# First cross attention of a decoder: batches in order, scores in three fp32r passes, splits and normalization on POOL

## The reference, cut to what matters

```
kv_rope = kv_c * cos + rotate_half(kv_c) * sin          # [8, 375, 128]
q_r = q_big @ W_qr ; k_r = kv_rope @ W_kr               # per head
scores = q_r @ k_r.T                                    # [8, 16, 112, 375]
attn = softmax(scores)
ctx_c = attn @ kv_rope                                  # [8, 16, 112, 128]
out = (ctx_c through w_kc_kv, per head) @ Wo.T
```

## Time and profile before

| | us |
|---|---|
| median of 3 runs | 1679.07 (1675.69, 1679.07, 1680.11) |
| the profiled execution | 1674.48 |
| its span, first to last instruction | 1672.7 |
| PE busy | 1604.6 (96%) |
| DVE busy | 989.6 (59%) |
| ACT busy | 730.5 (44%) |
| POOL busy | 508.7 (30%) |
| mean granted TensorE clock | 0.992 of 2.4 GHz |

### The profile page before, as it was taken

How to read it: one execution, slowest core, us unless ns; L and a number is a source line. 1 busy time by engine, 2 the same in 40 slices (tenths; PEclk the granted TensorE clock), 3 DMA queues, 4 the chain that set the end, 5 groups by cost and what they waited for, 6 DMA issues and landing times.

```text
span 1672.7 us, 24191 instructions
## 1 busy us (share of the span) xinstructions
PE 1604.6 (96%) x9704; PEld 1332.0 (80%) x9704; DVE 989.6 (59%) x1659; ACT 730.5 (44%) x1222; POOL 508.7 (30%) x335
## 2 busy tenths in 40 slices
PE   7999999999899999989999989999889999999998
PEld 7997667778688888867889987787668888888887
DVE  6555663455667675487758748244767455554554
ACT  2113664322577765666621146432635344353442
POOL 3875542620100002332118634111512432222321
PEclk9999999999899999999999999999999999999999
DMA  4110003133312004410001110111001111111111
GB/s 164 51 64 27 2 2 129 40 109 121 107 51 64 14 1 161 157 38 1 1 0 63 51 39 1 37 51 32 21 1 57 51 51 57 51 45 51 51 57 45
DMA packets 28579, 88.51 MB, mean 53 GB/s; under 512 B 4154, under 2 KB 4282, under 8 KB 28215
## 3 DMA queue, kind: packets, MB, share of 16 engines
q1 hardware_dynamic: 28468, 86.96, 15.5%
HBM read 85.11 MB, written 1.84 MB: 52 GB/s over the span
## 4 chain that ended last, share of the span: by engine, by line
PE 85%; DVE 8%; ACT 5%; issue 1%; POOL 0%; ACTq 0%; DVEq 0%
PE PS L255 17%; PE PS L257 17%; PE PS L256 17%; PE PS L260 6%; PE PS L1040 5%; PE PS L1058 4%; PE PS L1390 3%; PE PS L946 3%; PE PS L1405 2%; PE PS L555 2%; PE PS L579 1%; PE PS L1637 1%; PE PS L1625 1%; PE PS L545 1%; DVE sm L1659 1%
## 5 line engine op out<-in xcount | busy, mean ns | idle before, releaser
L301 POOL TENSOR_TENSOR HL<-stg,HL 128x1024 fp32r<-128x1024 f32 (+2 forms) x111 | 244.6, 2207 | 825.1 <-ACT HL L296 807.1
L255 PE MATMUL PS<-XT,HL 128*128 128x448 f32 x608 | 224.4, 369 | 4.3 <-DVE XT L336 3.7
L256 PE MATMUL PS<-XT,HL 128*128 128x448 f32 x608 | 222.6, 366 | 0.0
L257 PE MATMUL PS<-XT,HL 128*128 128x448 f32 x608 | 222.5, 366 | 0.0
L296 ACT ACTIVATE HL<-stg 128x1024 fp32r<-128x1024 f32 (+2 forms) x111 | 104.2, 944 | 216.0 <-PE PS L257 199.5
L255 PE MATMUL PS<-HL,XT 128*128 128x512 f32 (+1 forms) x380 | 137.5, 362 | 2.2 <-DVE XT L1909 1.4
L257 PE MATMUL PS<-HL,XT 128*128 128x512 f32 (+1 forms) x380 | 134.9, 355 | 0.0
L256 PE MATMUL PS<-HL,XT 128*128 128x512 f32 (+1 forms) x380 | 134.7, 355 | 0.0
L255 PEld LDWEIGHTS PS<-XT,HL 128*128 128x128 f32 x608 | 114.6, 188 | 16.5 <-DVE XT L336 4.9
L256 PEld LDWEIGHTS PS<-XT,HL 128*128 128x128 f32 x608 | 114.7, 189 | 9.1
L257 PEld LDWEIGHTS PS<-XT,HL 128*128 128x128 f32 x608 | 114.6, 188 | 9.2
(11 more groups left out here) (288 smaller groups left out, 3611.9 us busy)
## 6 DMA issues: line engine op xcount, KB each, us to landing
stg<-in_wst SPq DMA_DIRECT2D x87, 512.0 KB, 3.7
stg<-in_wst SPq DMA_DIRECT2D x16, 352.0 KB, 3.3
stg<-in_wst SPq DMA_DIRECT2D x16, 320.0 KB, 3.5
wsum<-in_wfc SPq DMA_DIRECT2D x8, 512.0 KB, 3.9
wsum<-in_wpj SPq DMA_DIRECT2D x8, 512.0 KB, 3.5
raw<-in_wfc SPq DMA_DIRECT2D x8, 512.0 KB, 7.9
stg<-in_wst SPq DMA_DIRECT2D x16, 256.0 KB, 2.8
raw<-in_wpj SPq DMA_DIRECT2D x7, 512.0 KB, 7.0
```

What stands on the lines that cost most here:

```text
L255: e.matmul(out, lh, rh, start=start, stop=False)
L256: e.matmul(out, lh, rl, start=False, stop=False)
L257: return e.matmul(out, ll, rh, start=False, stop=stop)
L301: e.tensor_tensor(slot(k)[:, 1, 0:n], stg[k % NSTG][:, 0:n], slot(k)[:, 0, 0:n].bitcast(F), A.subtract).then_inc(*done("pool_w", k))
```

## The change

The units go batch by batch: unit u is batch u // 8 and heads 2(u % 8), 2(u % 8) + 1. The result of a unit overwrites its own queries (`pair_of`), and queries no longer lie one slot above. The scores are three fp32r passes (`mm3`) of 376 columns (375 keys and one of zeros) in place of a plain fp32 matmul. For this POOL splits the queries of two units at a time (`query_parts`: a copy and a subtraction, 448 elements) and the keys of a batch (`keys_parts`: the same on 375). POOL also multiplies the exponentials by the reciprocal, both heads in one instruction with the reciprocal spread over 375 columns, which DVE did in two. The remainder of weight piece ox 2 is made by POOL in `pool_x` at step 3, behind the product of unit 2, where it was the last of `pool_q`. `pe_x` starts when the splits of batch 0 and of units 0 and 1 are there and the queries are all made; it no longer waits for the rotation of all batches before its first scores. The result pieces 0 to 3 are rounded and subtracted in two parts, batches 0 to 5 at steps 52 to 59, and batches 6 and 7 after the last unit.

```diff
+        QOX, KVX = rQO + 16 * 8 * S * 4, rKV + 24288
+        qxh = [at(f"qxh{i}", [128, 4, S], R, QOX + i * 3584) for i in range(2)]
+        qxl = [at(f"qxl{i}", [128, 4, S], R, QOX + i * 3584 + 1792) for i in range(2)]
+        kxh = [at(f"kxh{i}", [128, L + 1], R, (KVX + 6080, KVX)[i]) for i in range(2)]
+        kxl = [at(f"kxl{i}", [128, L + 1], R, (KVX + 3008, KVX + 1504)[i]) for i in range(2)]
...
         def qx_at(half, h):
-            s = 1 + 8 * (h // 8) + 4 * half
+            s = 8 * (h // 8) + 4 * half
...
             for b in range(NB):
                 rotate_rows(e, b)
-            for i in range(3):
+            for i in range(2):
+                e.tensor_scalar(kxh[i][:, L:L + 1], C("ones")[:, 0:1], 0.0, None, A.mult)
+                last = e.tensor_scalar(kxl[i][:, L:L + 1], C("ones")[:, 0:1], 0.0, None, A.mult)
+            last.then_inc(*done("pool_x", "pad"))
+            keys_parts(e, 0)
+            query_parts(e, 0)
+            for i in range(2):
                 rest_w(e, piece["ox", i][0])
...
+        def keys_parts(e, b):
+            e.wait_ge(*upon("dve_ctx", "k", b if b == 0 else NB - 1))
+            if b > 1:
+                e.wait_ge(*upon("pe_x", "sc", 8 * b - 9))
+            e.tensor_copy(kxh[b % 2][:, 0:L], kvT[:, b, :]).then_inc(*done("pool_x", "kh", b))
+            e.wait_ge(*upon("pool_x", "kh", b))
+            e.tensor_tensor(kxl[b % 2][:, 0:L], kvT[:, b, :], kxh[b % 2][:, 0:L].bitcast(F), A.subtract).then_inc(*done("pool_x", "k", b))
+
+        def pair_of(u):
+            return QO[:, 8 * (u // 4 % 2) + u // 8, 2 * (u % 4):2 * (u % 4) + 2, :]
+
+        def query_parts(e, u):
+            i = u // 2 % 2
+            q = QO[:, 8 * (u // 4 % 2) + u // 8, 4 * i:4 * i + 4, :]
+            if u < 8 or u == 32:
+                e.wait_ge(*upon("dve_q", "o", u + 1 if u < 8 else 7, u // 32))
+                e.wait_ge(*upon("act_q", "o", u + 1 if u < 8 else 7, u // 32))
+            if u > 3:
+                e.wait_ge(*upon("pe_x", "sc", u - 3))
+            e.tensor_copy(qxh[i][:, :, :], q).then_inc(*done("pool_x", "qh", u))
+            e.wait_ge(*upon("pool_x", "qh", u))
+            e.tensor_tensor(qxl[i][:, :, :], q, qxh[i][:, :, :].bitcast(F), A.subtract).then_inc(*done("pool_x", "q", u))
+
+        def pool_x(e):
+            for st in range(UX + 1):
+                if st % 2 == 0 and st + 2 < UX:
+                    query_parts(e, st + 2)
+                if st % 8 == 4 and st // 8 + 1 < NB:
+                    keys_parts(e, st // 8 + 1)
+                if st:
+                    u = st - 1
+                    k = u % 4
+                    e.wait_ge(*upon("dve_x", "rx", u))
+                    e.tensor_tensor(Sx[k][:, :, :], Sx[k][:, :, :], rx[:, k, :].unsqueeze(2).to_broadcast([S, 2, L]),
+                                    A.mult).then_inc(*done("pool_x", "p", u))
+                if st == 3:
+                    rest_w(e, piece["ox", 2][0])
...
         def pe_x(e):
-            e.wait_ge(*upon("dve_q", "o", 7, 1))
-            e.wait_ge(*upon("act_q", "o", 7, 1))
-            e.wait_ge(*upon("dve_ctx", "k", 7))
-            e.wait_ge(*upon("pool_ctx", "k", 7))
             for st in range(UX + 4):
                 if st < UX:
-                    b, bank = st // 4 % 8, 2 * (st % 2)
-                    if st > 1:
+                    b, bank = st // 8, 2 * (st % 2)
+                    if st % 8 == 0:
+                        e.wait_ge(*upon("pool_x", "k", b))
+                    e.wait_ge(*upon("pool_x", "q", st // 2 * 2))
+                    if st < 2:
+                        e.wait_ge(*upon("dve_q", "o", 7, 1))
+                        e.wait_ge(*upon("act_q", "o", 7, 1))
+                    else:
                         e.wait_ge(*upon("act_x", "exp", st - 2))
                     for e_ in range(2):
-                        last = e.matmul(PS[0:S, bank + e_, 0:L], QO[:, 1 + st // 4, 2 * (st % 4) + e_, :], kvT[:, b, :],
-                                        start=True, stop=True)
+                        i, j = st // 2 % 2, 2 * (st % 2) + e_
+                        last = mm3(e, PS[0:S, bank + e_, 0:L + 1], qxh[i][:, j, :], qxl[i][:, j, :], kxh[b % 2][:, :],
+                                   kxl[b % 2][:, :], True, True)
...
-                    e.wait_ge(*upon("dve_x", "p", u))
+                    e.wait_ge(*upon("pool_x", "p", u))
...
-                    ox_hi(e, (st - 52) // 2)
+                    ox_hi(e, (st - 52) // 2, 0)
                 if st == UX + 1:
                     value_hi(e, 0)
             value_hi(e, 1)
+            for c in range(4):
+                ox_hi(e, c, 1)
...
                     e.reciprocal(rx[:, k, :], sx[:, k, :]).then_inc(*done("dve_x", "rx", u))
-                    e.wait_ge(*upon("dve_x", "rx", u))
-                    for e_ in range(2):
-                        last = e.tensor_scalar(Sx[k][:, e_, :], Sx[k][:, e_, :], rx[:, k, e_:e_ + 1], None, A.mult)
-                    last.then_inc(*done("dve_x", "p", u))
...
             value_lo(e, 1)
             threshold(e)
+            for c in range(4):
+                ox_lo(e, c, 1)
...
+                    if c == 0 and t == 5:
+                        e.wait_ge(*upon("dve_ox", "lo", 0, 1))
```

More of the change, by code:

```diff
@@ L1056, in pe_x @@
                         e.wait_ge(*upon("dve_x", "o", u - 2))
+                    else:
+                        e.wait_ge(*upon("pool_ctx", "k", NB - 1))
                     for c in range(3):
-                        last = e.matmul(PS[:, 6 + u % 2, 0:2 * S], kvr[:, c, u // 4 % 8, :], PX[u % 2][:, :, c, :],
+                        last = e.matmul(PS[:, 6 + u % 2, 0:2 * S], kvr[:, c, u // 8, :], PX[u % 2][:, :, c, :],
                                         start=c == 0, stop=c == 2)
@@ L1110, in dve_x @@
                     e.reciprocal(rx[:, k, :], sx[:, k, :]).then_inc(*done("dve_x", "rx", u))
-                    e.wait_ge(*upon("dve_x", "rx", u))
-                    for e_ in range(2):
-                        last = e.tensor_scalar(Sx[k][:, e_, :], Sx[k][:, e_, :], rx[:, k, e_:e_ + 1], None, A.mult)
-                    last.then_inc(*done("dve_x", "p", u))
                 if 0 <= st - 4 < UX:
                     u = st - 4
-                    i = 2 * (u % 4)
                     e.wait_ge(*upon("pe_x", "pv", u))
-                    e.tensor_copy(QO[:, u // 4, i:i + 2, :],
-                                  PS[:, 6 + u % 2, 0:2 * S].rearrange("p (e s) -> p e s", e=2)).then_inc(*done("dve_x", "o", u))
+                    e.tensor_copy(pair_of(u), PS[:, 6 + u % 2, 0:2 * S].rearrange("p (e s) -> p e s", e=2)).then_inc(*done("dve_x", "o", u))
                 if st in (53, 55, 57, 59):
-                    ox_lo(e, (st - 53) // 2)
+                    ox_lo(e, (st - 53) // 2, 0)
                 if st == UX + 2:
@@ L1126, in dve_x, with ox_batches, ox_src, ox_part @@
             threshold(e)
+            for c in range(4):
+                ox_lo(e, c, 1)
         OX = 16
         first_ox = piece["ox", 0][0]
-        def ox_src(c):
-            return QO[:, 8 * (c // 8):8 * (c // 8) + 8, c % 8, :]
-        def ox_part(hl, c):
-            return XT[:, hl, c % 4, :].rearrange("p (b s) -> p b s", b=NB)
-        def ox_hi(e, c):
-            e.wait_ge(*upon("dve_x", "o", UX - 1 if c > 7 else UX // 2 - 1))
+        def ox_batches(c, part):
+            return (0, NB) if c > 3 else (6 * part, 6 + 2 * part)
+        def ox_src(c, part):
+            b0, b1 = ox_batches(c, part)
+            return QO[:, 8 * (c // 8) + b0:8 * (c // 8) + b1, c % 8, :]
+        def ox_part(hl, c, part):
+            b0, b1 = ox_batches(c, part)
+            return XT[:, hl, c % 4, :].rearrange("p (b s) -> p b s", b=NB)[:, b0:b1, :]
+        def ox_hi(e, c, part=1):
+            e.wait_ge(*upon("dve_x", "o", 8 * ox_batches(c, part)[1] - 1))
             if c > 3:
                 e.wait_ge(*upon("pe_ox", "c", c - 4))
-            else:
+            elif part == 0:
                 e.wait_ge(*upon("act_mag", 15))
-            e.activation(ox_part(0, c), ox_src(c), ACT.Copy).then_inc(*done("act_ox", "hi", c))
-        def ox_lo(e, c):
-            e.wait_ge(*upon("act_ox", "hi", c))
-            e.tensor_tensor(ox_part(1, c), ox_src(c), ox_part(0, c).bitcast(F), A.subtract).then_inc(*done("dve_ox", "lo", c))
+            e.activation(ox_part(0, c, part), ox_src(c, part), ACT.Copy).then_inc(*done("act_ox", "hi", c, part))
+        def ox_lo(e, c, part=1):
+            e.wait_ge(*upon("act_ox", "hi", c, part))
+            e.tensor_tensor(ox_part(1, c, part), ox_src(c, part), ox_part(0, c, part).bitcast(F),
+                            A.subtract).then_inc(*done("dve_ox", "lo", c, part))
         def value_bank(j):
@@ L1308, in pe_ox @@
                 if t == 1:
-                    e.wait_ge(*upon("dve_ox", "lo", OX - 1))
+                    e.wait_ge(*upon("dve_ox", "lo", OX - 1, 1))
                     e.wait_ge(*upon("dve_ox", "v", OX - 1))
```

(4 more changed lines are left out.)

4 lines of the change are left out of this document (2 added, 2 removed).

## The result

| | before | after |
|---|---|---|
| median, in runs on one chip | 1677.38 us, 6 runs (1673.92 to 1680.11) | 1669.27 us, 6 runs (1667.93 to 1670.28) |
| the profiled execution | 1674.48 us | 1670.28 us |
| its span | 1672.7 us | 1668.5 us |

After to before is 0.996, 95% interval 0.9945 to 0.9974: faster, by 0.26 to 0.55%. Forecast were 1672.9 us, a range of 1664 to 1682, and 6.2 us gained.

What follows compares the result with a forecast made beforehand. TensorE was taken to bound the cross attention stage at 3.05 us a unit, behind an opening of waits. Gain 13.6 us, less 6.9 (opening) and 0.5 (end), gives 6.2 us faster: 1672.9 us, 8-in-10 range 1664 to 1682.

Steps and rivals of the forecast that it cites:

- The scores: Layer 0 cross attention: six fp32r passes at 0.171 us replace four slow ones; unit 0.235 us shorter, 13.6 us over 58.
- DVE and ACT: Cross attention units: DVE loses 0.74 us of multiplications, worth nothing; ACT keeps 2.15 us, hidden under 2.82.
- POOL: Cross attention units: POOL's product and splits take 2.52 us, 89% of the 2.82 us unit, so hidden.
- The opening: Start of cross attention: moved remainder delays magnitude loads, ACT and TensorE stand 8 us; 6.9 us net lost (5.5 to 10).
- Scores 0 and 1 were to run at half clock: Opening of cross attention: these scores start at about 433.7 us and are done, at half clock, by 437.5.
- The end of the stage: After the last unit: ACT and DVE round and subtract the last two batches; nothing to about 1 us, 0.5 taken.
- The rival without a stall: Opening: first magnitudes land in time or POOL reaches the remainder 8 us earlier; opening gains about 1 us, 1665 us; 14%.
- The level: Whole kernel: 1668.3 us in the profiled execution's terms, carried to 1672.9 us by the 4.6 us to the median 1679.07.
- The chances: Whole kernel: faster 0.55, the same 0.32, slower 0.13, with 0.3% (5 us) about the limit told from no change.
- the same: Whole-kernel outcome within 0.3%: the rest of the forecast's 58% and a longer-stall rival at 1677 us (13%); put at 0.32.
- slower: Whole-kernel outcome: rivals of POOL becoming the bound (1698 us, 10%) and score passes saving nothing (1684, 5%); put at 0.13.

Runs made afterwards that it cites:

- Experiment 3: Changed kernel with its score passes in plain fp32 as before, POOL's splits and product kept: 1682.37 us, ratio to before 1.0037.
- experiment 4: Experiment 1 with the multiplication by the reciprocals back on DVE, POOL keeping the splits: 1660.08 us, ratio to before 0.9901.
- experiment 5: Experiment 1 with one more POOL pass in each unit that nothing needs (128x200 product): 1667.52 us, ratio to before 0.9944.
- Experiment 1: Changed kernel, but SP issues the first four loads of magnitudes ahead of the load waiting for the remainder of ox 2: 1659.68 us, ratio to before 0.9907.
- experiment 2: Changed kernel with only the remainder of ox 2 moved back to stage q, SP's order unchanged: 1659.55 us, ratio to before 0.9898.
- experiment 6: Experiment 1 plus 24 TensorE passes of no use behind scores 1, filling its wait: 1658.89 us, ratio to before 0.9896.
- experiment 7: Experiment 8 plus 12 TensorE passes of no use behind scores 1: 1656.81 us, ratio to before 0.9884.
- experiment 8: Changed kernel with magnitudes loaded before three waiting loads, units 2 and 3's query split in stage q, POOL's remainders after DVE's last rotation: 1657.30 us, ratio 0.9886.

## Why the prediction was right

- *The scores.* The step held exactly: 0.17 us a pass, from a line between the earlier trace rows, and 0.235 us a unit. Experiment 3 shows that the whole gain comes from it.
- *DVE and ACT.* DVE fell to 52% of the steady window and nothing followed; experiment 4 gives the work back, and nothing follows either.
- *POOL.* Forecast 2.52 us a unit at 89%, measured 2.40 at 85%: the product 1.44 us (forecast 1.43), the query copy 0.56 in 20 of the 24 of the steady window (0.55), the subtraction 1.14 (1.16). In the last four, which meet DVE's pass for the result pieces, the copy took 1.19 us. The sum was a little too high since a pass begins some 0.05 us before the one ahead of it ends, since the 0.08 us between a copy and its subtraction (which came as forecast) don't count as busy, and since the keys' subtraction took 0.91, not 1.0. The Trainium skill (GPSIMD Engine Reference, section 3.1, Elementwise side-by-side cycle accounting) would make the product 1.65 us, as an estimate from 4497 ns for 2048 elements; no run shows that, with 1440 ns for 750 elements and a spread operand, and the measurement decides. That this part was safe only by some 0.4 us (2.82 - 2.40) fits experiment 5, where 0.57 us more made POOL the bound.
- *The opening.* Forecast 6.9 us net. Unit 5's scores start 460.12 - 1.77 = 458.35 us on the clock of before, against 458.4 forecast and 451.46 before: 6.9. The chain came link by link, 1.7 to 1.8 us later throughout with the end of stage q: remainder done 450.49 (forecast 448.8), SP's loads 450.89 (449.2), ACT's sum 454.87 (453.1), transposes 1 456.78 (455.1). That it agrees to a tenth is partly luck: POOL came to the remainder 0.3 us late, having stood 0.44 us for the reciprocal of unit 2, and made it 0.3 us faster than forecast (1.53 us, not 1.82). Experiments 1 and 2 cut it at its two ends and find the same time, 1659.7 and 1659.6.
- *What failed in it.* Scores 0 and 1 were to run at half clock; with only 0.91 us without work ahead of them they ran at 1.00, 0.17 us a pass. It was scores 2 and 3, transposes 0 and the first pass of scores 4, after 4.48 us idle, that ran at half clock (0.51 in the window from 440.80). The faster scores 0 and 1 gained nothing, as DVE's maximum waited for the rotation of batch 7 (440.04 us), as forecast; the slow passes can have cost the chain at most the 0.44 us for which POOL stood before the product of unit 2. Measured to transposes 2 the opening costs 7.4 us (27.54 us after stage q's last matmul instead of 20.17), 0.5 us more than at unit 5's scores, since the half clock reaches into these (the window ends at 461.30).
- *The end of the stage.* Forecast 0.5 us, measured none: 13.6 - 7.4 = 6.2 is the whole of the stage's gain, and the first 120 matmuls behind the last transpose stand at the same distances from it in both traces, within 0.01 us. So the sum of 6.2 was met by luck in its last half microsecond: it was too much here and too little at the opening.
- *The rival without a stall* was put at 1665 us, 7.9 below the forecast. Experiment 1, which is that case, is 9.6 below the changed kernel, 9.5 by the stage. What the rival had too small was the gain of its opening, "about 1 us": unit 5's scores start 16.19 us behind the start of stage q's last matmul (448.40 - 432.21), where it was 18.90 before (451.46 - 432.56), so 2.7 us sooner, of which the unit of 3.34 us gives 0.6 back.
- *The level.* The forecast lies 3.6 us above the median measured. 1.7 us of that is the base, 1679.07 in the three runs of before and 1677.38 in the six; the other 1.9 is that the medians lie 8.1 apart where the stages lie 6.2, inside the scatter of the runs.
- *The chances.* Two are not quite what their terms give: the same, 0.17 + 0.13 = 0.30, where 0.32 stands, and slower, 0.10 + 0.05 = 0.15, where 0.13 stands. The forecast does not hang on it.

## What to carry to other kernels

Price a faster instruction by the distance between starts in an unbroken stretch of the nearest widths, and count each gain in units of the bound engine alone: here six fast passes a unit in place of four slow ones were worth 13.6 us, while, in the steady part, POOL's work of 2.40 us a unit more and DVE's of 0.74 less were worth nothing. Follow every step that is moved to the queues that wait for it: one remainder of 1.5 us, moved to spare 0.9, stood in front of a load, the load in front of sixteen others, and these in front of ACT, which cost 9.5 us. Put transfers that can go early ahead of those that wait for an engine's later work. And when a wait is taken away, look what is late next, before the one after it is tuned: in experiments 1, 6, 7 and 8 part of the gain was given back three units later, in a wait for POOL, until the product left it.

## What the runs showed of the hardware

- DVE's multiplication with one SBUF operand and a scalar for each partition, 112x375 fp32, is slowed by POOL too: 413 ns beside an idle POOL, 569 in the mean in experiment 4. In its timeline two take 0.74 us alone and 1.29 beside POOL's subtraction:

```profile
540.26 0.74 DVE L1163 TENSOR_SCALAR Sx<-Sx,rx 112x375 f32<-112x375 f32 x2
...
542.70 1.13 POOL L1061 TENSOR_TENSOR qxl<-QO,qxh 128x448 fp32r<-128x448 f32 x1
...
543.08 1.29 DVE L1163 TENSOR_SCALAR Sx<-Sx,rx 112x375 f32<-112x375 f32 x2
```

  The prediction had this only for passes with two SBUF operands. The Trainium skill (SBUF — State Buffer, section SBUF: two separate sides) says that such DVE passes, and those in a 2-port mode, share a port pair with POOL, locked for a whole instruction; the timeline agrees with a wait of that kind.
- POOL is slowed as well, and in the changed kernel's trace the pass that begins second mostly ends some 0.4 us behind the other engine's. POOL's first remainder ends at 437.91 us, DVE's pass of 1.80 us (else 0.55), begun at 436.51, at 438.32; POOL's second remainder (1.83 us, where 1.53 was enough at 448.96) at 439.71, DVE's next pass of 1.76 us at 440.12, POOL's query copy of 0.87 us (else 0.56) at 440.53. The copy is slowed to twice its time beside DVE's subtraction of a result piece:

```profile
605.28 1.14 DVE L1206 TENSOR_TENSOR XT<-QO,XT 128x672 fp32r<-128x672 f32 x1
605.65 1.19 POOL L1059 CAST qxh<-QO 128x448 fp32r<-128x448 f32 x1
```

- In the changed kernel the granted clock stayed at 1.00 through a gap of 0.91 us and fell to 0.50 in the gap of 4.48 us. In experiment 1 TensorE was then busy without a gap for 5.2 us (the first window shown for experiments 6 and 7) and still at 0.50. In experiment 8 the clock fell as well, behind a gap of 2.01 us and while TensorE had no idle time (the window's length, then TensorE's busy time):

```profile
441.00:444.40 3.40, 3.40 (x15) 3.32 (x14) 2.02 (x4) 2.09 (x6) 3.32 (x4) 0.50 0.37 133
```
